# Mamba mixer with routed experts on one core: the D-skip term moved into PSUM, the state's operand built by GpSimd

## The reference, cut to what matters

```python
zxbcdt = x @ W_in                              # z, then x/B/C (convolved, silu), then dt
def step(h, inp):                              # per token, 8 heads of 64 channels, state of 128
    dti, xi, Bi, Ci = inp
    dA = jnp.exp(dti * A)
    h = h * dA[:, :, None, None] + dti[:, :, None, None] * xi[..., None] * Bi[:, None, None, :]
    y = jnp.einsum('bhpn,bn->bhp', h, Ci)
    return (h, y)
y = scan(step) + D_skip[None, None, :, None] * xh        # the skip term: D of the head times x
y = y * silu(z);  y = y * rsqrt(mean(y * y) + EPS) * rms_w;  y @ W_out
```

## Time and profile before, and how to read it

| | before |
|---|---|
| median of 3 executions | 1944.52 us (1940.91 to 1946.15) |
| span of the profiled execution | 1934.6 us |
| PE busy in it | 1609.3 us (83%) |
| DVE busy | 1323.2 us (68%) |
| ACT busy | 1107.9 us (57%) |
| POOL busy | 982.6 us (51%) |
| mean granted TensorE clock | 0.954 of full speed |

### The profile page before, as it was taken

The page is one execution under the profiler, slowest core; times in us unless marked ns, Lnnn a source line. Parts: engine busy times, 40 slices in busy tenths (PEclk is TensorE's granted clock), DMA queues, the critical chain, the costliest instruction groups (busy, mean ns, idle before and its releaser), DMA issues. The chain is left out here.

```text
span 1934.6 us, 35851 instructions
## 1 busy us (share of the span) xinstructions
PE 1609.3 (83%) x10690; PEld 1343.0 (69%) x10690; DVE 1323.2 (68%) x3304; ACT 1107.9 (57%) x2311; POOL 982.6 (51%) x940
## 2 busy tenths in 40 slices
PE   6749999999999999999999886258888787786798
PEld 4337777777777777777777775147778777776565
DVE  6647788888888888888888776524444444443588
ACT  4535767676767676676767565435555545554222
POOL 2103345565565656565655556735555555555443
PEclk9869999999999999999999998579999999999899
DMA  8620111121121222121221113755555455552998
GB/s 280 213 73 22 38 35 57 60 73 66 65 74 59 69 70 70 61 79 58 71 69 62 66 49 109 233 153 157 153 160 168 148 166 158 157 155 87 355 400 321
DMA packets 149272, 237.88 MB, mean 123 GB/s; under 512 B 27788, under 2 KB 96140, under 8 KB 148912
## 3 DMA queue, kind: packets, MB, share of 16 engines
q1 hardware_dynamic: 123200, 165.83, 27.3%
q0 software_dynamic: 25344, 69.50, 9.7%
q10 hardware_dynamic: 544, 0.26, 0.0%
HBM read 128.28 MB, written 109.35 MB: 123 GB/s over the span
## 5 line engine op out<-in xcount | busy, mean ns | idle before, releaser
L2141 POOL DMA_INDIRECT ys_dram<-byo,bids x272 | 260.9, 959 | 256.4 <-DVE bids L2121 156.7
L1580 DVE SCALAR_TENSOR_TENSOR cv<-xc,convw,cv 128x256 f32<-128x256 f32 x576 | 300.1, 588 | 14.2 <-ACT cv L1421 13.9
L1055 POOL DMA_INDIRECT xs_dram<-rows,dest x256 | 267.5, 1045 | 77.6 <-issue 74.4
L115 PE MATMUL bank<-wh,bhh 128*128 x544 | 161.5, 297 | 78.1 <-ACT bhh L2046 67.5
L2094 DVE TENSOR_TENSOR bhl<-bank,bhh 128x512 fp32r<-128x512 f32 x136 | 94.1, 692 | 192.5 <-ACT bhh L2046 181.5
L2046 ACT ACTIVATE bhh<-bank 128x512 fp32r<-128x512 f32 x136 | 83.5, 614 | 182.2 <-PE bank L1979 173.0
L115 PEld LDWEIGHTS bank<-wh,bhh 128*128 128x128 f32 x544 | 103.5, 190 | 91.4 <-issue 91.3
L116 PE MATMUL bank<-wl,bhh 128*128 x544 | 154.4, 284 | 1.4 <-issue 1.4
L117 PE MATMUL bank<-wh,bhl 128*128 x544 | 154.2, 284 | 0.8 <-issue 0.8
L115 PE MATMUL bank<-hTh,win_hi 128*128 128x256 f32 x384 | 115.4, 301 | 16.7 <-POOL hTl L1823 10.5
L1270 PE MATMUL bank<-xdt,dec 128*128 128x64 f32 x1024 | 122.6, 273 | 5.7 <-DVE dec L1606 5.7
(11 more groups left out here) (272 smaller groups left out, 5268.9 us busy)
## 6 DMA issues: line engine op xcount, KB each, us to landing
bx<-xs_dram SPq DMA_DIRECT2D x272, 129.0 KB
cy<-ys_dram SPq DMA_DIRECT2D x32, 1024.0 KB, 12.8
px<-in_x SPq DMA_DIRECT2D x16, 512.0 KB, 5.4
h_t<-phT SPq DMA_DIRECT2D x16, 512.0 KB, 3.6
hT<-h_t SPq DMA_DIRECT2D x32, 256.0 KB
xr<-in_x SPq DMA_DIRECT2D x32, 256.0 KB
x_dram<-xr SPq DMA_DIRECT2D x32, 256.0 KB, 2.0
h_dram<-h SPq DMA_DIRECT2D x32, 256.0 KB
```

The costliest lines, as they stand in the source:

```text
L115: pe.matmul(out, a_hi, b_hi, start=start, stop=False, skip_group_check=True)
L1055: pool.indirect_dma_start(out=xs_dram[:, :], out_offset=bass.IndirectOffsetOnAxis(ap=dest[p][:, CH * b + c, k:k + 1], axis=0), in_=rows[b] ...
L1580: dve.scalar_tensor_tensor(cv[b][:, m, :], xc[b][:, m, tap:tap + GROUP], convw[:, m, tap:tap + 1], cv[b][:, m, :], ALU.mult, ALU.add).then ...
L2141: pool.indirect_dma_start(out=ys_dram[:, :], out_offset=bass.IndirectOffsetOnAxis(ap=ids[u % XBUF][:, n:n + 1], axis=0), in_=yo[u % YBUF][ ...
```

## The change

It takes D as a row of eight values on every partition (`skip_w` is now 128x8) instead of four diagonal matrices; it leaves the turned x in PSUM, lets VectorE multiply it by D in place, and lets TensorE add the products with the decays onto that. The four fp32 matmuls of each chunk go. The state's operand `xend` is now made by GpSimd from `xdt` (in SBUF), times the decay alone, so parameter 3 no longer holds dt. The cut diff:

```diff
-        dcol = sb("dcol", [P, KI])
-                    for m in range(KI):
-                        dve.tensor_scalar(skip_w[:, m, :], ident[:, :], dcol[:, m:m + 1], None, ALU.mult)
-                    dve.tensor_tensor(pars[b][:, :, 3, :], steps(dt[b]), steps(s2[b]), ALU.mult).then_inc(pars_done, 1)
+                    dve.tensor_copy(pars[b][:, :, 3, :], steps(s2[b])).then_inc(pars_done, 1)
-        skip_w = sb("skip_w", [P, KI, P])
+        skip_w = sb("skip_w", [P, H])
+        skip_done = sems("skip_done", CH)
...
                 def x_by_token(b, i, c):
-                        last = pe.transpose(Q(b, c)[:, m * P:(m + 1) * P], cv[b][:, m, c * P:(c + 1) * P],
-                                            ident[:, :])
+                        last = pe.matmul(Q(b, c)[:, m * P:(m + 1) * P], cv[b][:, m, c * P:(c + 1) * P], ident[:, :],
+                                         start=(m == 0), stop=False, is_transpose=True, skip_group_check=True)
...
                 def within(b, i, c):
                     pe.wait_ge(xdt_done[b], CH * i + c + 1)
-                    pe.wait_ge(xend_done[b], CH * i + c + 1)
-                    for m in range(KI):
-                        pe.matmul(Q(b, c)[:, m * P:(m + 1) * P], cv[b][:, m, c * P:(c + 1) * P], skip_w[:, m, :],
-                                  start=(m == 0), stop=False, skip_group_check=True)
+                    pe.wait_ge(skip_done[b], CH * i + c + 1)
                     pe.wait_ge(w_done[b], CH * i + c + 1)
...
                 def squares(b, i, c):
                     act.wait_ge(y4_done[b], CH * i + c + 1)
+                    act.wait_ge(xend_done[b], CH * i + c + 1)
...
-                def times_end(b, i, c):
+                def times_skip(b, i, c):
                     dve.wait_ge(xT_ps[b], CH * i + c + 1)
-                    dve.wait_ge(add_ps[b], CH * i)
-                    dve.wait_ge(ag_done[b], i)
-                    dve.tensor_tensor(xend[b][:, c, :].rearrange("p (h e) -> p h e", h=H),
-                                      Q(b, c)[:, :].rearrange("p (h e) -> p h e", h=H),
-                                      par[b][:, 3, c, :].unsqueeze(2).to_broadcast([P, H, HD]),
-                                      ALU.mult).then_inc(xend_done[b], 1)
+                    dve.wait_ge(xdt_done[b], CH * i + c + 1)
+                    x = Q(b, c)[:, :].rearrange("p (h e) -> p h e", h=H)
+                    dve.tensor_tensor(x, x, skip_w[:, :].unsqueeze(2).to_broadcast([P, H, HD]),
+                                      ALU.mult).then_inc(skip_done[b], 1)
...
                             times_dt(*second, c)
-                            times_end(*second, c)
+                            times_skip(*second, c)
...
+                def times_end(b, i, c):
+                    pool.wait_ge(xdt_done[b], CH * i + c + 1)
+                    pool.wait_ge(par_in[b], 16 * (i + 1))
+                    pool.wait_ge(add_ps[b], CH * i)
+                    pool.wait_ge(ag_done[b], i)
+                    pool.tensor_tensor(xend[b][:, c, :].rearrange("p (h e) -> p h e", h=H),
+                                       xdt[b][:, c, :].rearrange("p (h e) -> p h e", h=H),
+                                       par[b][:, 3, c, :].unsqueeze(2).to_broadcast([P, H, HD]),
+                                       ALU.mult).then_inc(xend_done[b], 1)
...
                     if tail:
                         shift_x(*tail)
+                    if second:
+                        times_end(*second, 0)
+                        times_end(*second, 1)
                     if sent:
                         scatter(pool, *sent, slice(2, 8))
```

More of the change, by code:

```diff
@@ L225, in prepare_tokens @@
         consts = [(w_dt[:, :, ROWS_DT - H:ROWS_DT], "W_dt"), (rms, "rms_w"), (upto, "upto"), (after_raw, "after"), (far_raw, "far"), (convw, "conv_w"),
-                  (convb, "conv_b"), (dtb, "dt_bias"), (negA, "A_log"), (dcol, "D_col"), (glub, "glu_b")] + route_consts
+                  (convb, "conv_b"), (dtb, "dt_bias"), (negA, "A_log"), (skip_w, "D_row"), (glub, "glu_b")] + route_consts
         CONSTS = 16 * len(consts)
@@ L2392, in host_layout @@
         "A_log": everywhere(a["A_log"], H),
-        "D_col": columns(np.repeat(a["D_skip"], HD)),
+        "D_row": everywhere(a["D_skip"], H),
         "glu_b": columns(a["glu_b"]),
```

## The result

The changed kernel takes 2003.1 us (median of four, 1999.8 to 2006.5), the kernel before 1943.9 us in the same comparison: ratio 1.030, 95% interval 1.027 to 1.033. It is slower by 59 us where 41 were forecast. That is inside the range for 8 in 10 (1955 to 2018), but 1 us above the forecast's own range (1970 to 2002), and between the two rivals with a dearer outcome (the port at 2000, the clock at 2009). First the page of the changed kernel: its span, the busy time of each engine, and in the last line the granted TensorE clock in tenths over 40 slices.

What follows compares the result with a forecast made beforehand. The prediction took a loop through VectorE and GpSimd, not TensorE, to bound the scatter halves. Its terms, -1 + 41.7 + 1 - 1 = +41 us, added to 1944.5 gave 1985.5; range for 8 in 10, 1955 to 2018.

Steps and rivals of the forecast that it cites:

- the port: Rival: in choose, both new GpSimd operations block VectorE, making it 2.34 us late; odd halves lose 15 us more, 2000; chance 0.15.
- the clock: Rival: growing idle time lowers TensorE's clock, costing one us per half on the chain, 24 us more, 2009; chance 0.10.
- The chain through VectorE and GpSimd: In the scatter halves, new state, scatters and decayed state form a loop setting the period; removing TensorE's matmuls gains 0 there.
- TensorE is the bound: Rival: TensorE, 92% busy, sets the period, so the removed matmuls save up to 67 us, giving 1877; chance 0.12.
- gain and loss cancel: Rival: the extra GpSimd time is hidden by slack behind VectorE's 1.41 us idle and little is gained, 1944.5; chance 0.08.
- Early halves: Five halves without scatters, where the removed matmuls reach VectorE by 0.24 us each, about -1 us.
- VectorE's own delay: In choose, 0.26 us plus a blocked operation of some 0.9, less than GpSimd's cost there; in assign, inside VectorE's idle time.
- The wait for itself: VectorE's times_skip waits for its own xdt_done, about 0.13 us per chunk, 0.26 per half.
- GpSimd's two operations: Ahead of the six scatters and decayed state, 2.4 us per half; after subtracting GpSimd's waits and adding step 16, +41.7 us.
- over 3 us: Sign of being right: in the even half VectorE's new_state 0 waits over 3 us for the decayed state.
- The other sign that failed: Sign of being right: TensorE's busy time falls by about 60 us while the kernel's time rises.
- The 1.24 us of GpSimd's waiting: In the odd half GpSimd waits 1.24 us for from_state 0, which was to absorb half of its 2.4 us.

Runs made afterwards that it cites:

- the experiment with the gap: The changed kernel with GpSimd's times_end for chunk 1 moved from ahead of the six scatters to ahead of gate_y 0, where GpSimd waits; 2042.0 us, ratio 1.050.

## Why the prediction was right, and what it mis-sized

**The outcome.** Slower, as forecast, for the reason forecast, but by 59 us and not by 41, and that it came so near is partly luck. In the traces the difference is 69, and a cost of 37 us was left out of the sum.

**The bound.** Right. The chain through VectorE and GpSimd sets the period, not TensorE at 92%: the skip matmuls alone taken away bring nothing (even halves 32.55 for 32.31), two scatters moved give 65 us back. (The same move gives the kernel before 19 to 31 us too, so not all of the 65 are the change's.) The rival "TensorE is the bound" (0.12) is refuted, "gain and loss cancel" (0.08) too.

**Early halves.** -0.24 us each forecast for five; measured 30.90 to 30.62, -0.28, in the first three. The fourth, the first with choose, went from 33.17 to 35.47 us and the fifth from 31.25 to 32.04. No scatter stands in them, so VectorE's own delay (T to N +0.95 in both) reached the chain at its full length, and in the fourth the clock came on top. So the five together cost 2 us instead of giving 1.

**times_skip.** 0.68 us taken, 0.70 measured (0.698 to 0.700 in all 64, GpSimd's shift_x beside some of them), so writing PSUM in place costs VectorE next to nothing. The wait for itself was taken as 0.13 us per chunk; the starts of the two times_skip are 1.39 us apart, those of the two times_end of before were 1.19, so it costs 0.2, some 0.4 per half. T to Y grew by 0.92 us in even halves and 0.71 in odd ones, which holds this wait and the blocked operations; 0.26 + 0.9 had been forecast. That VectorE's delay is hidden under GpSimd's was right for this kernel. Its price without that cover is seen in the two mixers with late scatters: 17 of the 23 us between them lie in T to N.

**GpSimd's two operations.** 2.4 us taken, bounds 2.0 and 2.9; the pair takes 2.25, and T to N of the even half grew by 2.07 (median). In the odd half 1.1 were forecast, 0.89 measured. Twelve of each are 36 us, against the forecast's sum of 41.7. (These are medians; added up half by half, T to N of the 24 grew by 32 us, since in the kernel before some odd halves were already as late as 14.4.) VectorE's wait for the decayed state came to 2.68 us, not 3.8: of the 2.25 us it had itself used 0.92 up ahead of the wait. The number named as a sign ("over 3 us") forgot that its own term for VectorE applies in this half too. The other sign that failed is TensorE's busy time: it was to fall by 60 us and rose by 30, which is the clock.

**The step that failed is TensorE's clock.** It stood among the rivals, at 0.10, as something that happens instead of the forecast, at one us per half: 24 us and 2009. By the sign named for it, a granted clock under 1.00 between 400 and 1000 us, this rival came true: the clock is 0.91 there, where it was 1.00 before. It is a term of the sum. From gated to gated the odd half was forecast at 34 us and is 33.92 (median), the even one at 35.7 and is 37.9; where the even halves had their needless matmuls, and so their clock, it is 35.34. So without the clock the forecast was right to 0.4 us per half. The term itself: even halves 12 x 2.06 = 25 us; three of the twelve odd halves took 38.2 us where the others take 34.9 (the granted clock is 0.50 from 631 to 640 us, behind new_state 0 of the first of them), and the last of the 30 halves has its project_out 1.5 us late, together some 11; the first half with choose 1.3 (N to X 6.26 for 4.93). That is about 37 us, and with the 36 above they make the 71.5, within some 2 us, which the small terms on both sides make. Of these 37 us only the 25 of the even halves rest on an experiment; the others are read off the trace. The forecast's total came near by luck: the GpSimd term was 6 us too high, and the traced execution of before was shorter than the timed ones, which takes 10 us off the difference as the medians show it. The clock's cost was left out of the sum with all of its 37 us.

It could have been seen from the prediction's own numbers: it wrote that idle time would grow to 6 us of 35, and had a row in which the clock fell beside much idle time. What it left out is that TensorE has from_state 1 and within 1 to do between the stall and the projection, and the projections between that and the next chain: at doubled durations the former last beyond xo_done (N to X 4.78 to 5.88 us), and X to O goes from 7.64 to 9.15.

**The port in choose** (0.15) did not decide: T to Y in odd halves grew by 0.71, not 2.34. It did act in assign, on an operation with two SBUF inputs (L1029: 1.15 us beside times_end, 0.42 in the kernel before), and in the experiment with the gap it decided.

**What the chip adds.** The 1.24 us of GpSimd's waiting that the forecast took off in each odd half belongs to the chip of that trace. On the others the odd half of before has no such play: T to N is 12.75 there, while in the changed kernel's order it is 14.50 on either. The 30 halves of before took 974 us on the third chip and 994 in the first trace, while the odd halves in the changed kernel's order are alike on two chips (35.80 and 35.84). By these rows (an estimate, since the changed kernel itself was not run there) the change costs 20 us more on such a chip: with the 24 us that the needless matmuls gained added to the 1869 of that kernel, about 1893 us to before's 1801.

**Open.** Why TensorE's signals, by the modelled ends of its matmuls, reach the other engines late in odd halves on one chip; and why three odd halves of twelve lose their clock at the start of this stretch and the others don't, though T to N is 14.50 us in both.

## What to carry to other kernels

Where the waits form a loop through two engines, work taken off a third is worth nothing, and an operation put into the loop costs its length wherever the loop has no play (here 2.07 of 2.25 us in even halves, 0.89 in odd ones). The cheapest gain here was to move what nobody waits for (the scatters: 0.984 on one chip and 0.996 on another, with no operation removed) behind what somebody waits for. A stall given to TensorE has a second price: price the work behind it at 1.2 GHz as a term of the sum, and ask whether that work ends on the chain. By the experiment with the gap, a free slot on GpSimd is free only if no VectorE operation with two SBUF inputs runs there.

## What was not expected of the hardware

- Needless matmuls made the mixer faster: eight in each even half with routing work, 24 us less, with a clock of 0.98 instead of 0.89 (600 to 800 us).
- A VectorE operation of 1.22 us takes 2.07 when it starts 0.04 us behind a GpSimd operation of 1.03 us.
- Scatters issued by GpSimd beside VectorE operations: 1.44 and 1.68 us, 0.96 usual. Between 300 and 1100 us their maximum is 1.68 in the kernel with xend by GpSimd alone and 1.49 in the kernel before, so part of it is not new. In that stretch of these two kernels and of the changed one, the 155 scatters that run beside no VectorE TENSOR_TENSOR or SCALAR_TENSOR_TENSOR on SBUF operands alone take 1.01 us at most. Of the 382 that do run beside one, half take more than 1.05 us, up to the 1.68. By the Trainium skill, "SBUF — State Buffer", section on who interferes with whom, a `tensor_tensor` takes only the read side of the shared pair, and it is inferred there that making descriptors is not held up. These rows speak against that, but no run was made to separate the two.
- The same program, the kernel before, takes 1942 to 1947 us in the first comparisons and 1800 and 1801 on two other chips, and not only the experts' stage differs: busy shares of 1250 to 1700 us, first trace and then the third chip (columns as above):

```profile
1250.00:1700.00 450.00, 344.72 (x2754) 329.20 (x2754) 193.53 (x581) 223.56 (x573) 228.32 (x233) 0.96 0.52 158
```

```profile
1250.00:1700.00 450.00, 418.10 (x3392) 407.09 (x3393) 240.80 (x705) 297.56 (x697) 279.38 (x282) 0.96 0.67 212
```

TensorE is busy for 345 us there and for 418 here, at the same clock; the transfers move 158 and 212 GB/s. A ratio measured on one chip carries over to another only where the stage in question behaves alike on both.
